# Packing half chunks of two feed-forward weights into one, and adding three biases outside TensorE

## The reference

```python
q = _heads(hidden_states @ q_w.T + q_b, b, s)
k = _heads(hidden_states @ k_w.T + k_b, b, s)
v = _heads(hidden_states @ v_w.T + v_b, b, s)
qp = elu(q) + 1.0
kp = elu(k) + 1.0
kv = einsum('bhsd,bhse->bhde', kp, v)
z = einsum('bhsd,bhd->bhs', qp, kp.sum(axis=2))[..., None]
attn = einsum('bhsd,bhde->bhse', qp, kv) / (z + EPS)
out = attn.transpose(0, 2, 1, 3).reshape(b, s, HID) @ o_w.T + o_b
...
x1 = _bitlinear(x, w1)      # w1, w2: 704 x 256, w3: 256 x 704
x2 = _bitlinear(x, w2)      # _bitlinear: x @ quantize(w).T, values -1, 0, 1
return _bitlinear(sigmoid(x1) * x2, w3)
```

## Time and profile before

| | |
|---|---|
| median of 3 runs | 431.73 us (431.62 to 432.14) |
| profiled execution | 434.08 us, its span 432.3 us |
| busy: PE, DVE, ACT, POOL | 384.6, 294.3, 205.9, 129.5 us |
| first phase, about | 0 to 140 us |
| expert phase, about | 140 to 243.8 us |
| last phase | 243.8 us to the end |
| slot 5 of it, block_out to block_out | 348.11 to 368.17 us |

### The profile page before, as it was taken

The page is one execution under the profiler, slowest core; times in us unless marked ns, Lnnn a source line. Parts: engine busy times, 40 slices in busy tenths (PEclk is TensorE's granted clock), DMA queues, the critical chain, the costliest instruction groups (busy, mean ns, idle before and its releaser), DMA issues.

```text
span 432.3 us, 7368 instructions
## 1 busy us (share of the span) xinstructions
PE 384.6 (89%) x2260; PEld 332.9 (77%) x2260; DVE 294.3 (68%) x789; ACT 205.9 (48%) x419; POOL 129.5 (30%) x226
## 2 busy tenths in 40 slices
PE   3999999999739889999999868999999999999691
PEld 3888888888627677777777657988889889999690
DVE  4787999999982456687453255676868686866532
ACT  3374586558652433345335414554455544636341
POOL 2002256444632430003201167234435240401111
PEclk9999999999867999999999985999999999999977
DMA  6543954211122345733431131102020100000000
GB/s 210 184 172 127 137 207 146 70 37 50 49 76 94 99 153 150 247 98 100 134 111 50 52 94 52 50 0 74 4 72 27 49 27 2 24 2 25 2 26 24
DMA packets 28486, 35.70 MB, mean 83 GB/s; under 512 B 3680, under 2 KB 25632, under 8 KB 28192
## 3 DMA queue, kind: packets, MB, share of 16 engines
q1 hardware_dynamic: 19760, 21.72, 17.3%
q0 software_dynamic: 3072, 8.39, 6.0%
q10 hardware_dynamic: 5616, 5.11, 3.4%
HBM read 22.76 MB, written 12.45 MB: 81 GB/s over the span
## 4 chain that ended last, share of the span: by engine, by line
PE 49%; DVE 33%; issue 7%; ACT 6%; POOL 2%; another core or an unknown queue 1%; DMA 1%; SPq 0%; ACTq 0%; POOLq 0%; DVEq 0%
PE bank L394 20%; PE bank L535 10%; PE bank L556 8%; DVE st L1017 4%; PE bank L662 3%; PE bank L545 2%; PE bank L515 2%; PE bank L404 2%; DVE arena L1079 2%; PE bank L717 2%; DVE arena L1082 2%; DVE arena L1059 1%; DVE fl L1421 1%; DVE arena L1450 1%; DVE arena L1355 1%
## 5 line engine op out<-in xcount | busy, mean ns | idle before, releaser
L394 PE MATMUL bank<-arena 128*128 128x256 f32 (+2 forms) x576 | 120.2, 364 | 9.5 <-ACT arena L792 6.7
L394 PEld LDWEIGHTS bank<-arena 128*128 128x128 f32 x576 | 102.0, 195 | 23.4 <-issue 6.7
L778 ACT ACTIVATE arena<-bank 128x256 f32<-128x256 f32 (+1 forms) x118 | 45.5, 424 | 47.7 <-PE bank L556 26.4
L1538 POOL TENSOR_TENSOR ve<-mv,eps 128x2 f32<-128x2 f32 x32 | 7.0, 219 | 165.9 <-DVE mv L1021 165.9
L535 PE MATMUL bank<-gu,arena 128*128 x156 | 54.9, 476 | 0.0
L556 PE MATMUL bank<-dn,arena 96*128 x156 | 41.0, 385 | 4.6 <-DVE arena L1238 3.5
L783 ACT ACTIVATE arena<-arena,nm,rs 128x256 f32<-128x256 f32 x48 | 26.2, 597 | 38.7 <-POOL nm L1543 38.6
L1604 POOL DMA_INDIRECT arena<-yg,ypos x32 | 31.3, 978 | 39.0 <-DMA yg<-arena 30.6
L1238 DVE COPY arena<-bank 96x256 f32<-96x256 f32 x39 | 16.3, 419 | 39.1 <-PE bank L545 31.6
L556 PEld LDWEIGHTS bank<-dn,arena 96*128 96x128 f32 x156 | 28.7, 190 | 15.1 <-issue 7.0
L1578 POOL DMA_INDIRECT xg<-x,pos x32 | 34.3, 1073 | 14.7 <-issue 7.5
(11 more groups left out here) (207 smaller groups left out, 866.1 us busy)
## 6 DMA issues: line engine op xcount, KB each, us to landing
arena<-xg SPq DMA_DIRECT2D x39, 128.0 KB, 2.1
yg<-arena ACTq DMA_DIRECT2D x39, 128.0 KB
arena<-in_xT SPq DMA_DIRECT2D x8, 256.0 KB
x<-in_x SPq DMA_DIRECT2D x8, 256.0 KB, 4.4
out<-arena SPq DMA_DIRECT2D x8, 256.0 KB
gu<-in_w_gate SPq DMA_DIRECT2D x1, 1408.0 KB, 8.2
gu<-in_w_up SPq DMA_DIRECT2D x1, 1408.0 KB, 6.9
dn<-in_w_down SPq DMA_DIRECT2D x11, 128.0 KB, 6.0
```

The source lines that it names most:

```text
L394: last = pe.matmul(dst, l, r, start=i == 0, stop=i == len(pairs) - 1)
L778: return act.activation(dst, src, ACT.Copy)
```

## The change

Five edits:

1. The sixth chunk of w1q takes the last 64 columns of W1 in its first half and those of W2 in its second. w2q ends after five chunks. ternary 2 leaves out the sixth chunk of w2q (12 matmuls in place of 16). For that chunk tanh_half writes to the upper 64 partitions of fb, gate_times multiplies there, f_high keeps the high part in the upper half of fh and f_low puts the low part in its lower half; W3's last 64 rows are loaded twice, and ternary_out 2 takes one matmul for each token half there (6 in place of 8). The four steps of pair 2 are two instructions each.
2. The keys' bias: biased_keys on VectorE, between block_out and combined, adds it to K and writes kp; key_exponents and keys read kp.
3. The values' bias: mask_kv adds, by two further instructions after the mask, the product of the masked bias and the sum of the keys (a column of the same bank). The masked bias (value_bias) is made once, in `prepare`.
4. The output's bias: bias_residual on GpSimd, first in its slot, adds it to x2 once that is turned; attention_residual waits for it.
5. `pick`, `biases` and the instructions that made them are gone; the sum over W3 is two reductions, the first over 64 partitions and six chunks, the second over the other 64 and five.

```diff
@@ SyncE @@
-                    sp.wait_ge(w3z_ok, 1)
                     last = HID // P
                     sp.dma_start(raw3[:, 0:last, :], chunked(W3[0:last * P, :])).then_inc(in_w3, 16)
-                    sp.dma_start(raw3[0:HID - last * P, last, :], W3[last * P:HID, :]).then_inc(in_w3, 16)
+                    for p0 in (0, LEFT):
+                        sp.dma_start(raw3[p0:p0 + LEFT, last, :], W3[last * P:HID, :]).then_inc(in_w3, 16)
@@ TensorE @@
                     for i in range(2):
+                        if w is w2q and 2 * p + i == NF - 1:
+                            continue
...
-                        for q, l in enumerate((fh, fl)):
+                        for q, l in enumerate((fh, fl) if f < NF - 1 else (fh,)):
...
-                        last = product(halves(dst)[:, t, :], [(pick[:, :], biases[:, cols])] + [
+                        last = product(halves(dst)[:, t, :], [
...
-                pe.wait_ge(kvm_ok, s + 1)
+                pe.wait_ge(kvm_ok, 2 * (s + 1))
...
-                    last = product(halves(BANK_O)[:, t, :], [(pick[:, :], biases[:, 2 * C:3 * C])] + [
-                        (anT[:, k, chunk(t)], wo3[:, k, :]) for k in range(KC)])
+                    last = product(halves(BANK_O)[:, t, :], [(anT[:, k, chunk(t)], wo3[:, k, :]) for k in range(KC)])
@@ ScalarE @@
-                if i == 7:
-                    act.wait_ge(in_bias, 48)
-                    copy(bias_hi[:, :], bias_raw[:, :])
-                    copy(biases[0:64, :], bias_raw[0:64, :]).then_inc(bias_hi_ok, 1)
...
+                if p < NPAIR - 1:
+                    last = act.activation(fb[n % 2][:, :, :], src, ACT.Tanh, scale=0.5)
+                else:
+                    act.activation(fb[n % 2][:, 0, :], src[:, 0, :], ACT.Tanh, scale=0.5)
+                    last = act.activation(fb[n % 2][LEFT:P, 1, :], src[0:LEFT, 1, :], ACT.Tanh, scale=0.5)
...
+                    copy(fh[:, n % 2, 0, :], fb[n % 2][:, 0, :])
+                    last = copy(fh[LEFT:P, n % 2, 1, :], fb[n % 2][LEFT:P, 1, :])
...
-                act.wait_ge(kp_ok, s + 1)
-                past(act, kvs_ok, s)
-                act.activation(ek[:, :, :], halves(BANK_K), ACT.Relu, scale=-1.0).then_inc(nk_ok, 1)
+                act.wait_ge(kb_ok, s + 1)
+                act.activation(ek[:, :, :], kp[:, :, :], ACT.Relu, scale=-1.0).then_inc(nk_ok, 1)
@@ VectorE @@
-                    dve.wait_ge(in_w3, 32)
-                    dve.tensor_reduce(wsum[:, 2:3], raw3[:, :, :], mybir.AxisListType.XY, ALU.add,
-                                      apply_absolute_value=True).then_inc(wsum_ok, 1)
+                    dve.wait_ge(in_w3, 48)
+                    for rows_of, n in ((slice(0, LEFT), NF), (slice(LEFT, P), NF - 1)):
+                        last = dve.tensor_reduce(wsum[rows_of, 2:3], raw3[rows_of, 0:n, :], mybir.AxisListType.XY, ALU.add,
+                                                 apply_absolute_value=True)
+                    last.then_inc(wsum_ok, 1)
...
+                    parts = ([(w1q[:, k, 0:HID], slice(0, HID))] if j == 0 else
+                             [(w2q[:, k, :], slice(0, whole)), (w1q[:, k, HID:], slice(whole, HID))])
...
+                    dve.scalar_tensor_tensor(f[:, 0, :], f[:, 0, :], 1.0, second[:, 0, :], ALU.add, ALU.mult)
+                    last = dve.scalar_tensor_tensor(f[LEFT:P, 1, :], f[LEFT:P, 1, :], 1.0, first[LEFT:P, 1, :],
+                                                    ALU.add, ALU.mult)
...
+                    dve.tensor_tensor(fl[:, n % 2, 0, :], fb[n % 2][:, 0, :], fh[:, n % 2, 0, :].bitcast(F32),
+                                      ALU.subtract)
+                    last = dve.tensor_tensor(fh[0:LEFT, n % 2, 1, :], fb[n % 2][LEFT:P, 1, :],
+                                             fh[LEFT:P, n % 2, 1, :].bitcast(F32), ALU.subtract)
...
+            def biased_keys(s):
+                dve.wait_ge(kp_ok, s + 1)
+                past(dve, kvs_ok, s)
+                dve.tensor_tensor(kp[:, :, :], halves(BANK_K), key_bias[:, :].unsqueeze(1).broadcast_to([P, NT, C]),
+                                  ALU.add).then_inc(kb_ok, 1)
...
-                dve.scalar_tensor_tensor(kp[:, :, :], halves(BANK_K), 1.0, ek[:, :, :], ALU.add,
+                dve.scalar_tensor_tensor(kp[:, :, :], kp[:, :, :], 1.0, ek[:, :, :], ALU.add,
...
+                dve.tensor_tensor(kvm[:, :, :], kv[:, :, 0:KVW], msk[:, :, :], ALU.mult).then_inc(kvm_ok, 1)
+                dve.wait_ge(kvm_ok, 2 * s + 1)
+                for k in range(KC):
+                    one = P * (KC - 1 - k)
+                    last = dve.scalar_tensor_tensor(kvm[:, k, :], value_bias[:, k, :], kv[:, k, one:one + 1],
+                                                    kvm[:, k, :], ALU.mult, ALU.add)
+                last.then_inc(kvm_ok, 1)
...
                 dve.wait_ge(o3_ok, s + 1)
+                dve.wait_ge(x2b_ok, s + 1)
...
                 if s >= 2:
                     block_out(s - 2)
+                if attn:
+                    biased_keys(s)
                 if 1 <= s < B - 1:
                     combined(s + 1)
@@ GpSimd @@
-            pool.memset(pick[:, :].bitcast(F32), 0.0).then_inc(pick_ok, 1)
-            pool.memset(w1q[:, :, HID:].bitcast(F32), 0.0)
-            pool.memset(w2q[:, :, HID:].bitcast(F32), 0.0).then_inc(pick_ok, 1)
...
+            def bias_residual(b):
+                pool.wait_ge(x2Tp_ok, b + 1)
+                if b == 0:
+                    pool.wait_ge(in_bias, 48)
+                pool.tensor_tensor(x2[b % 2][:, :, :], x2[b % 2][:, :, :],
+                                   out_bias[:, :].unsqueeze(1).broadcast_to([P, NT, C]), ALU.add).then_inc(x2b_ok, 1)
+
             for s in range(B + 2):
+                if s < B:
+                    bias_residual(s)
                 if s >= 2:
                     deviation(3, s - 1)
```

More of the change, by code:

```diff
@@ L23 @@
 NPAIR = NF // 2
+LEFT = HID % P
 HEAD = 16
@@ L227, in build @@
         qtmp = then(NF, C)
-        bias_raw = then(3 * C)
+        bias_raw = then(C)
+        place[0] += 2 * C
         yy = [then(NT, 2, C) for _ in range(2)]
@@ L944, in f_high @@
                 past(act, w3_ok, n - 1)
-                copy(fh[:, n % 2, :, :], fb[n % 2][:, :, :]).then_inc(fh_ok, 1)
+                if p < NPAIR - 1:
+                    last = copy(fh[:, n % 2, :, :], fb[n % 2][:, :, :])
+                else:
+                    copy(fh[:, n % 2, 0, :], fb[n % 2][:, 0, :])
+                    last = copy(fh[LEFT:P, n % 2, 1, :], fb[n % 2][LEFT:P, 1, :])
+                last.then_inc(fh_ok, 1)
             def x3_high(b):
```

74 lines of the change are left out of this document (43 added, 31 removed).

## The result

The changed kernel took 445.1 us in the median (443.94 to 445.86, four runs) against 431.68 us for the kernel before beside it. The ratio is 1.0312, with a 95% interval of 1.0291 to 1.0333. It is slower by 13.4 us, and the prediction had 437.5, with a range up to 441.0: the direction was right, the size less than half of what came.

What follows compares the result with a forecast made beforehand. VectorE was taken to bound a slot up to attend, then TensorE up to attention_out, then ScalarE and VectorE. Expert phase 0.8, slots 0 and 1 0.6, middle slots 4.4, slots 7 and 8 0.0 gave +5.8: 437.5 us, range 432.8 to 441.0.

Steps and rivals of the forecast that it cites:

- Together +0.6: Slots 0 and 1: +0.1 us for slot 0 and +0.5 for slot 1, including GpSimd's addition holding combined in slot 1.
- 0.24 + 0.62 - 0.85 = 0.0: Slot 7: ScalarE's first wait 0.24 us later, longer mask 0.62, less the 0.85 gained behind attend; no net change.
- hold 0.5: Middle slots, ahead of attend: GpSimd's addition blocks VectorE's combined, costing about 0.5 us, bounds 0 and 1.26.
- Rival 1: GpSimd's addition holds nobody, saving 0.5 us in five slots and 0.9 in slot 1: 434.1 us; chance 0.20.
- rival 2: All of TensorE's savings are time, 1.61 us a slot, with no wait at attend: 419.6 us; chance 0.14.
- A gain of 0.85: Behind attend: ternary_out 2 starts 0.61 us earlier and is 0.24 shorter; bounds 0.6 and 1.13.
- For the others I estimate 0.06 to 0.1 above the one piece: Pair 2 behind attend: halved tanh, f_high and f_low take 0.66, 0.70, 0.79 us; ternary_out 2 starts 9.62 after attend's start A.
- halves at full price: Behind attend: lower bound of the gain, 0.6 us, if each half piece of pair 2's steps costs full price.
- +0.1: Slot 0: query_limits' wait for TensorE ends 0.48 us earlier, the mask costs 0.62; +0.1 in all.
- rival 3: TensorE's clock falls inside the slots, its pauses making ternary 1 dearer, 11 us in seven slots: 448.6 us; chance 0.06.
- the median ... is 431.73, 2.35 less. So a profiled run of 439.9 and a median of 437.5: Last step: the median stays 2.35 us below the profiled run, 434.08 for the kernel before and 439.9 for the changed one.
- +0.8: Expert phase: two reductions over W3 delay the copy hidden_turned, which TensorE's down projection awaits, by 0.8 us; bounds 0 and 1.4.

Runs made afterwards that it cites:

- late: Changed kernel with GpSimd's output-bias addition moved: for block 0 ahead of the gathers, otherwise behind the second chain of statistics; nothing left out. Ratio to the kernel before 1.016.
- no_value: Changed kernel with the values' bias left out, so the mask stands alone without its two further pieces. Ratio to the kernel before 1.0153.
- no_out: Changed kernel without GpSimd's addition of the output bias, which is left out. Ratio to the kernel before 1.0152.
- again: The kernel before, unedited, run and profiled once more. Measured 428.46 us, ratio 0.9999.
- before_warm2: The kernel before with unread extra matmuls in two TensorE waits, at the end of slot 7 and between slots 7 and 8. Ratio to the kernel before 0.9996.
- after_again: The changed kernel, unedited, run once more beside others of its group. Ratio to the kernel before 1.029.
- pack_only: The kernel before with the packing alone (halved steps of pair 2, two sums over W3); all biases stay on TensorE. Ratio to the kernel before 1.0018.
- one_sum: Changed kernel with a single reduction over W3, counting the doubled rows twice, so its threshold scale is wrong. Ratio to the kernel before 1.0234.
- bias_only: Changed kernel without the packing (whole pieces, one sum over W3); the three biases are off TensorE. Ratio to the kernel before 1.0258.
- both fillings: Unread extra matmuls, 16 in slot 7's wait and 12 between slots 7 and 8. Ratios: packing alone 0.9972, packing with output bias 0.9959, changed kernel 1.0258.

## Why the prediction was right in direction and short in size

The step that failed is the part of the sum outside the middle slots: "Together +0.6" for slots 0 and 1, "0.24 + 0.62 - 0.85 = 0.0" for slot 7 and "0" for the last one, and with them the step from the profile to the median. The runs showed 2.3 to 2.7, 0.9 to 1.4 and 0.1 to 1.7 us in their place. By the two profiles of record the change costs 9.9 us, 4.1 more than the sum of 5.8. By the medians it costs 13.4: the profiled execution lies 2.35 above the median in the kernel before and 1.2 below it in the changed one, which is another 3.5. About 2 of these are the clock at the end of slot 7 and in slot 8, as below; the other 1.5 stay open.

- **Ahead of attend: right.** 10.31 forecast, 10.34 measured (10.30 to 10.34 in slots 2 to 6), and its parts: hold 0.5 (late takes 0.48 away), biased_keys 0.58 against 0.61, mask pieces 0.67 against 0.62 (attend starts 364.89 - 363.73 = 1.16 behind the mask, 356.69 - 356.20 = 0.49 in the kernel before; no_value gives 0.68). Rival 1, no hold, is refuted by late, rival 2, all of TensorE's savings as time, by the wait of 0.90 at attend.
- **Behind attend: right in kind, too large.** A gain of 0.85 was taken; slots 5 and 6 gained 0.53. The term that was mis-sized is "For the others I estimate 0.06 to 0.1 above the one piece": they came 0.17 to 0.21 above. The four steps took 0.77, 0.85, 0.84 and 0.86, 3.3 in all, against 2.6 as whole pieces and 3.0 forecast: ternary_out 2 began at A + 9.93, not 9.62. The bound "halves at full price" was given, and would have said 0.6. Slots 2 to 4 gained 0.93, since they had been 0.6 longer there before (12.1 against 11.5), which was not looked at. Over the five slots the errors cancel in part: 4.4 forecast, 4.9 to 5.0 measured.
- **Slots 0 and 1: the mechanism was known and not carried there.** The sum had "+0.1" for slot 0, with nothing for GpSimd's addition. It holds combined for 1.5 us there, and GpSimd's next deviation and gather wait for the statistics behind it. In slot 1 the forecast had the hold (0.9) and it was 0.4 to 0.9. Together 2.3 to 2.7 in place of 0.6. In no_out, without the addition, the slots from the first product to the first block_out took 40.6 us, and in the kernel before 40.3 to 41.7; in late, with the addition moved, 42.0. The sum took the half clock of slot 1 as one profile had it, and its length varies. TensorE runs at 1.2 GHz for about 3, 6 and 13 us of these two slots in three profiles of the kernel before (again, before_warm2, the one of record), for about 10, 10 and 17 in those of the changed one, and for 6 in no_out. At a like 10 us (after_again, late, pack_only) the two slots take 43.2, 42.0 and 40.6 us, so moving the addition is worth 1.1; how much of the rest is the longer chain and how much the clock wasn't tested.
- **Slot 7: not 0.** "GpSimd's addition meets nothing with two SBUF inputs" holds, but attend came 9.16 after block_out against 8.10, so 1.06 later where 0.86 was forecast, and behind it only 0.2 was gained (12.47 to 12.30) where 0.85 was taken. So the gain of the middle slots was wrongly carried over. pack_only shows it by itself: in slot 7 it has attend 0.35 later (8.44 against 8.09 in again) and gains nothing behind it (12.45 against 12.46). That attention_out stands ahead of ternary 2 in this slot is the likely reason, which no run tested. Part of the 1.4 in the second pair is the clock, which fell before the end of the slot.
- **Slot 8 and the clock: rival 3 looked in the wrong place.** It had the fall inside the slots of the middle; the clock stayed at 1.00 there (20 us windows of slots 2 to 6, all kernels). It came at the end of slot 7, where the earlier trace rows had already shown a fall in the profile of record. That profile was taken as the rule. The two later profiles of the kernel before (again and before_warm2) don't have that fall, and all three of the changed kernel do. That most executions are like these is likely from the medians of the mean clock, 0.961 to 0.965 and 0.943 to 0.950, but not shown: the stretch in slots 0 and 1 moves the mean as well. The fall is worth 1.7 us between the two profiles of one chip, and up to 3 (12.61 against 15.65) in others. What failed here is the last step of the sum, "the median ... is 431.73, 2.35 less. So a profiled run of 439.9 and a median of 437.5": it took the whole distance between profile and median as common to both kernels, while some 2 us of it was this stretch, which the profile of the kernel before already had.
- **The expert phase: the step was right** (+0.8; the wait is 0.77, and gone in one_sum). The phase as a whole came 1.0 to 1.7 later; profiles of the kernel before alone differ by 1.8 there, so no more can be said.

In numbers, from 5.8 to the 11.8 of the second pair: slots 0 and 1 +2.1, slot 8 +1.7, slot 7 +1.4, slots 2 to 6 +0.6, expert phase +0.2. The medians of these two kernels differ by 12.4 us, the ones of record by 13.4; the last 0.6 to 1.6 us are not accounted for by stage.

## What to carry to other kernels

Price a hold at each place where the two engines can meet, the first slots above all: here a steady slot lost 0.5 us to it and the first one 1.5. Taking work off the engine that is busiest only pays where that engine is what the next step waits for; elsewhere it makes idle time, and at the end of the program this idle time cost about as much in clock as the packing had saved. Before a profile's end is used as the reference, see from several executions whether its slow stretch is there in most of them.

## What the runs showed that had not been expected

- Operations on half the partitions cost what whole ones do: 0.42 us for 64x256 and for 128x256 on VectorE, 0.38 for both on ScalarE, 3.23 for two reductions of 64 partitions against 1.74 for one of 128.
- VectorE's operation with two SBUF inputs can be held longer than GpSimd's operation lasts: 1.98 against a usual 0.48 beside an addition of 1.27, though VectorE had begun 0.4 us earlier by its record. In slot 0 of bias_only it had begun 0.6 earlier (258.22 and 258.83) and took 2.17.
- With the same two idle waits, 1.84 or 1.85 and 2.04 us, the clock fell in one execution of the kernel before and not in another; with about 0.7 and 0.6 (three kernels with both fillings, the packed ones and the changed one) slot 8 was at 2.4 GHz throughout each time.
